# A two-block transformer on one core: the next batch's routed-row attention moved beside the causal attention's first half, and the second MLP beside the second half's maxima

## The reference, cut to what matters

```python
h = _layernorm(x) * (1 + ca) + sa
x = x + ga * (light_attn(h) + scatter(null_token, idx_q, heavy_attn(h[idx_q], h[idx_kv])))
h = _layernorm(x) * (1 + cb) + sb
x = x + gb * (einsum(relu(s[..., None] * W1 + b1), W2) + b2) @ Wout      # s = h @ Win + bin
h = _layernorm(x) * (1 + ca1) + sa1
x = x + ga1 * causal_attention(h)       # q, k normalised per head, rotary, softmax, 16 heads of 16
h = _layernorm(x) * (1 + cb1) + sb1
x = x + gb1 * (gelu(h @ bw1.T + b1) @ bw2.T + b2)                        # binarised weights
```

## Time and profile before

| | us |
|---|---|
| median of three runs | 5111.87 |
| the profiled execution's own time | 5113.72 |
| its span, first to last instruction | 5112.0 |
| TensorE matmul busy | 3773.6 (74%) |
| VectorE (DVE) busy | 2667.1 (52%) |
| ScalarE (ACT) busy | 2000.5 (39%) |
| GpSimd (POOL) busy | 1505.8 (29%) |
| mean granted TensorE clock | 0.854 of full |

### The profile page before, as it was taken

How to read it: one execution, slowest core, us unless ns; L and a number is a source line. 1 busy time by engine, 2 the same in 40 slices (tenths; PEclk the granted TensorE clock), 3 DMA queues, 4 the chain that set the end, 5 groups by cost and what they waited for, 6 DMA issues and landing times. The chain is left out here.

```text
span 5112.0 us, 59839 instructions
## 1 busy us (share of the span) xinstructions
PE 3773.6 (74%) x19064; PEld 2104.3 (41%) x19064; DVE 2667.1 (52%) x7124; ACT 2000.5 (39%) x4464; POOL 1505.8 (29%) x1900
## 2 busy tenths in 40 slices
PE   2014956789768877788768977789768977789777
PEld 1012633346333553346433543346333543346333
DVE  3845454635645364635645364636545364636542
ACT  0040433344425443345425443345425443345433
POOL 0611333124331343114321343114321343114311
PEclk7556968899779987899779988899779988899789
DMA  4200012100220013100120012100220012100220
GB/s 139 90 27 27 11 38 68 29 12 19 45 70 13 19 38 68 29 12 19 45 70 13 19 38 68 29 12 19 45 70 13 19 38 68 29 12 19 45 51 5
DMA packets 207220, 191.49 MB, mean 37 GB/s; under 512 B 12825, under 2 KB 189081, under 8 KB 206874
## 3 DMA queue, kind: packets, MB, share of 16 engines
q1 hardware_dynamic: 189378, 161.19, 12.8%
q10 hardware_dynamic: 14208, 18.09, 1.0%
q0 software_dynamic: 3328, 8.39, 0.6%
HBM read 121.99 MB, written 65.11 MB: 37 GB/s over the span
## 5 line engine op out<-in xcount | busy, mean ns | idle before, releaser
L2120 ACT ACTIVATE arena<-pb 128x512 f32<-128x512 f32 (+3 forms) x1536 | 679.2, 491 | 683.4 <-PE pb L1375 678.6
L2203 POOL TENSOR_TENSOR arena<-arena,small 128x512 f32<-128x512 f32 x256 | 279.8, 1094 | 641.1 <-DVE small L1553 638.8
L1952 ACT ACTIVATE arena<-arena,small 128x256 f32<-128x256 f32 x512 | 256.0, 500 | 451.2 <-DVE small L1536 451.1
L2361 POOL TENSOR_SCALAR_AFFINE_SELECT arena<-arena 128x256 f32<-128x256 f32 x512 | 212.2, 419 | 711.7 <-ACT arena L2120 708.3
L1375 PE MATMUL pb<-arena 98*128 98x512 bf16 (+3 forms) x1152 | 355.1, 352 | 81.4 <-DMA arena<-nullv_nmr 50.5
L1392 PE MATMUL pb<-arena,v 128*17 128x512 f32 (+3 forms) x3072 | 384.1, 513 | 22.6 <-POOL arena L2361 12.7
L1823 DVE TENSOR_REDUCE arena<-pb 128x1 f32<-128x512 f32 x512 | 328.4, 681 | 103.6 <-PE pb L1350 103.5
L1815 DVE TENSOR_REDUCE arena<-pb 128x4 f32<-128x512 f32 x256 | 174.3, 691 | 371.8 <-PE pb L1341 366.9
L1089 PE MATMUL pb<-arena 128*128 128x256 f32 x1024 | 291.3, 409 | 11.8 <-issue 6.3
L1536 DVE CUSTOM_DVE_ANT_0 arena<-pb,wmask 128x256 f32<-128x256 f32 x512 | 195.9, 419 | 198.7 <-PE pb L1089 152.1
L1066 PE MATMUL pb<-hTf,wqkv 128*128 128x512 f32 (+1 forms) x640 | 262.4, 553 | 35.8 <-issue 22.9
(11 more groups left out here) (340 smaller groups left out, 7889.1 us busy)
## 6 DMA issues: line engine op xcount, KB each, us to landing
split_q<-arena SPq DMA_DIRECT2D x384, 64.0 KB
arena<-split_q SPq DMA_DIRECT2D x64, 384.0 KB, 4.5
split_k<-arena SPq DMA_DIRECT2D x192, 64.0 KB
arena<-split_k SPq DMA_DIRECT2D x24, 384.0 KB, 15.9
arena<-in_x SPq DMA_DIRECT2D x8, 1024.0 KB, 7.7
h_d<-arena ACTq DMA_DIRECT2D x8, 1024.0 KB, 4.4
xn<-h_d SPq DMA_DIRECT2D x8, 1024.0 KB
xt<-in_x SPq DMA_DIRECT2D x16, 512.0 KB, 3.9
```

Source lines behind the costliest of these rows:

```text
L1952: ins = s.activation(pm[n % 3][:, j], sm[n % 2][:, j], ACT.Exp, bias=nmx[:, 2 * sl + j:2 * sl + j + 1], scale=-1.0, accum_out=sml[:, 2 * s ...
L2120: s.activation(pp[pn % 4][:, h % 2, 0:w_], bank[n % 3][:, 0:w_], ACT.Exp).then_inc(a_exp1, 1)
L2203: g.tensor_tensor(pm[n % 3], pm[n % 3], rcl[:, 2 * sl:2 * sl + 2].unsqueeze(2).broadcast_to([P, 2, 2 * P]), ALU.mult).then_inc(p_norm0, 1)
L2361: g.affine_select(out=p2, in_=p2, pattern=[[0, 2], [1, P]], compare_op=ALU.is_ge, fill=0.0, base=0, channel_multiplier=-1).then_inc(p_tri, 1)
```

## The change

It moves stages in the planner and adapts what they wait for:

- lane 1 takes heavy of batch b+1 directly after chain 2, ahead of mlp1 of the first half, gated on chain 3's end; heavy gets 71 steps instead of 61;
- while heavy is under way beside att, lane 0's pace is 0.28 (PACE_BESIDE_HEAVY); otherwise 0.5 beside the first half and 1.0 beside the second (before 0.9 and 0.8);
- the second half may begin without mlp1 of the first half; hnorm starts at att step 45 instead of 1;
- the gathers leave mlp1 and stand at heavy's start on GpSimd, one a step, behind the wait for chain 3's last part; heavy's waits for the MLP's last products go;
- the loads of the second half's first two head groups leave chain 3's end and att's start, and stand at key tile 2 of groups 2 and 3 of the first half.

Stepping the new `schedule()` gives for a middle batch: chains 2 and 3 end at att steps 11 and 19 of the first half; heavy stands beside steps 20 to 37 and the first 2 of the second half; mlp1 of the first half beside steps 3 to 27 (the fills); hnorm beside 53 to 62; mlp1 of the second half beside the next light, as before. In batch 0 heavy's ten more steps stand beside light, ahead of the chains.

```diff
-    "heavy": 61, "chain": 42, ("mlp1", 0): 25, ("mlp1", 1): 24, "hnorm": 10,
+    "heavy": 71, "chain": 42, ("mlp1", 0): 25, ("mlp1", 1): 24, "hnorm": 10,
-PACE = {("light", 0): 1.5, ("light", 1): 1.0, ("att", 0): 0.9, ("att", 1): 0.8}
+PACE = {("light", 0): 1.5, ("light", 1): 1.0, ("att", 0): 0.5, ("att", 1): 1.0}
+PACE_BESIDE_HEAVY = 0.28
...
-        lanes[1] += [("heavy", b, 0)] * (b == 0) + [("chain", b, 0), ("chain", b, 2), ("mlp1", b, 0)]
-        lanes[1] += [("heavy", b + 1, 0)] * (b + 1 < B) + [("mlp1", b, 1)]
+        lanes[1] += [("heavy", b, 0)] * (b == 0) + [("chain", b, 0), ("chain", b, 2)]
+        lanes[1] += [("heavy", b + 1, 0)] * (b + 1 < B) + [("mlp1", b, 0), ("mlp1", b, 1)]
-            gate["hnorm", b, 0] = [(("att", b - 1, 1), 1)]
+            gate["hnorm", b, 0] = [(("att", b - 1, 1), 45)]
+            gate["heavy", b, 0] = [(("chain", b - 1, 3), 42)]
-        gate["att", b, 1] = [(("chain", b, 2), 42), (("chain", b, 3), 42), (("mlp1", b, 0), 14)]
+        gate["att", b, 1] = [(("chain", b, 2), 42), (("chain", b, 3), 42)]
...
+            if lanes[0][0][0] == "att" and lanes[1] and lanes[1][0] in done and lanes[1][0][0] == "heavy":
+                pace = PACE_BESIDE_HEAVY
...
                 def heavy(b, _):                      # DVE
                     if b:
-                        v.wait_ge(t_w2, TH * (2 * b - 1))
-                        v.wait_ge(p_w2, TH * (2 * b - 1))
-                        v.wait_ge(split_out[1][1], 16 * SPLIT_DMAS * b)
+                        v.wait_ge(split_out[1][0], 16 * SPLIT_DMAS * b)
...
+                    if b:
+                        v.wait_ge(p_chain[1], nth(CHAIN_P, 2 * b - 1, "lo1"))
...
                 def gather(b):                        # GpSimd
+                    if b:
+                        g.wait_ge(split_out[1][0], 16 * SPLIT_DMAS * b)
+                        g.wait_ge(p_chain[1], nth(CHAIN_P, 2 * b - 1, "lo1"))
...
                 def heavy(b, _):
+                    yield from gather(b)
                     g.wait_ge(gate01_in, 16 * (b + 1))
                     if b:
-                        g.wait_ge(t_w2, TH * (2 * b - 1))
                         g.wait_ge(split_out[1][1], 16 * SPLIT_DMAS * b)
...
-                    if c == 0 and b + 1 < B:          # GpSimd, mlp1
-                        g.wait_ge(t_n2, 4 * b + 2)
-                        g.wait_ge(p_chain[1], nth(CHAIN_P, 2 * b + 1, "lo1"))
-                        gather(b + 1)
...
-                    if q == 3:                        # SyncE, chain
-                        load_group(b, 1, 0)
...
-                        if c == 0 or g > 0:           # SyncE, att
+                        if c == 0 or g == 2:
                             load_group(b, c, g)
...
+                            if c == 0 and g >= 2 and kt_ == 2:
+                                load_group(b, 1, g - 2)
```

More of the change, by code:

```diff
@@ L102, in schedule @@
             gate["start", b, 0] = [(("hnorm", b, 0), 10)]
-            gate["hnorm", b, 0] = [(("att", b - 1, 1), 1)]
+            gate["hnorm", b, 0] = [(("att", b - 1, 1), 45)]
+            gate["heavy", b, 0] = [(("chain", b - 1, 3), 42)]
         for q in range(4):
             light = ("light", b, q // 2)
-            gate["chain", b, q] = [(("heavy", b, 0), 61), (light, steps_of(light) - (2 if q % 2 else 18))]
+            gate["chain", b, q] = [(("heavy", b, 0), steps_of(("heavy", b, 0))), (light, steps_of(light) - (2 if q % 2 else 18))]
             if b:
@@ L126, in turn @@
             return
-        if key[0] == "chain" and key[2] == 3 and n == 41 and not reached([(("chain", key[1], 2), 42), (("att", key[1], 0), 22)]):
+        if key[0] == "att" and key[2] == 0 and n == NEXT_KEYS and not reached([(("chain", key[1], 2), 42), (("chain", key[1], 3), 42)]):
             return
-        if key[0] == "light" and key[1] > 0 and key[2] == 0 and n == LOAD_STEP and not reached([(("heavy", key[1], 0), 61)]):
+        if key[0] == "light" and key[1] > 0 and key[2] == 0 and n == LOAD_STEP and not reached([(("heavy", key[1], 0), steps_of(("heavy", key[1], 0)))]):
             return
@@ L1136, in heavy @@
                 def heavy(b, _):
-                    yield
-                    yield
+                    for _ in range(12):
+                        yield
                     for j in range(4):
@@ L1981, in heavy @@
                 def heavy(b, _):
-                    yield
-                    yield
+                    for _ in range(12):
+                        yield
                     if b:
-                        s.wait_ge(p_w2, TH * (2 * b - 1))
                         s.wait_ge(split_out[1][1], 16 * SPLIT_DMAS * b)
@@ L2239, in heavy @@
                     yield
-                    for j in range(4):
+                    for j in range(6):
                         yield
@@ L2449, in heavy @@
                     load_gates(b, 0, 2, gate01_in)
+                    for _ in range(11):
+                        yield
                     sp.wait_ge(p_const, 2 * b + 1)
                     sp.dma_start(heavy_d.rearrange("(t p) d -> p t d", p=P), nullg.unsqueeze(1).broadcast_to([P, T, D])).then_inc(fill_in, 16)
-                    for _ in range(60):
+                    for _ in range(59):
                         yield
@@ L2490, in chain @@
                     yield
-                    if q == 3:
-                        load_group(b, 1, 0)
-                        if b + 1 < B:
-                            for j_ in range(2):
-                                sp.wait_ge(t_chain[j_], nth(CHAIN_T, n, "p_n2"))
-                            sp.dma_start(xn[:, :, :], h_d[(b + 1) * N:(b + 2) * N, :].rearrange("(t p) d -> p t d", p=P)).then_inc(in_h, 16)
+                    if q == 3 and b + 1 < B:
+                        for j_ in range(2):
+                            sp.wait_ge(t_chain[j_], nth(CHAIN_T, n, "p_n2"))
+                        sp.dma_start(xn[:, :, :], h_d[(b + 1) * N:(b + 2) * N, :].rearrange("(t p) d -> p t d", p=P)).then_inc(in_h, 16)
                     yield
```

7 lines of the change are left out of this document (5 added, 2 removed).

## The result

| | before | after |
|---|---|---|
| median, us | 5112.63 (5106.52 to 5113.86) | 5299.35 (5288.02 to 5315.81, 4 runs) |
| ratio to before | | 1.037, 95% interval 1.034 to 1.040 |
| profiled execution, us | 5113.72 | 5315.81 |
| TensorE busy, us | 3773.6 | 3905.6 |
| mean granted clock | 0.854 | 0.842 |

The change costs 187 us where 112 were forecast. The median lies 4 us above the forecast's own range (5165 to 5295) and 11 inside the range of 8 in 10 (5040 to 5310).

The account below looks back on a forecast made before the run. Outside the score steps, waits inside stages and program order bound a batch. -54.7 - 7 + 78 = +16.3 us a middle batch, seven +114, batch 7 -7, batch 0 +4: +111, 5225 us; own range 5165 to 5295, 8 in 10 5040 to 5310.

Parts of the forecast that it names:

- Second half: Second half of a middle batch: heavy and hnorm leave, -54.7 us; second MLP beside the fills, -7 us.
- Chains at double pace: First half up to att step 19: 75 us, with chain turns at 1.08 us each wherever they stand.
- Prelude: Heavy's gathers to transposes beside att steps 20 to 23 of the first half: 17 us, those steps hidden.
- Projections: Heavy's six rotations in the first half with four att steps half hidden beside them: 24 us.
- Rounds with heavy's end: Heavy's sixteen full rounds at 3.7 us, trailing rounds, projections and the attention's last steps in the first half: 76 us.
- Light: The light stage of each batch: not touched by the change, so no cost was forecast.
- Heavy fits the first half as well as the second: Rival, 28%: beside att steps 20 to 37 the move costs +55 us, not +78; kernel about 5060 us.
- The MLP gains nothing: Rival, 5%: program order holds MLP and fills, so their -7 us a batch becomes 0; kernel 5280 us.
- everything waits in turn: Rival, 9%: in the first half nothing of heavy is hidden, or half clock; +111 us, kernel 5450 us.
- wrong if rounds came under 4 us apart: Sign against the forecast: heavy's head rounds in the first half standing less than 4 us apart.
- 4.5 to 5 us apart: Expected sign: spacing of heavy's head rounds in the first half, against 6.5 us before the change.

Follow-up runs that it names:

- experiment 4: Kernel before with chains 2 and 3 at pace 0.5 instead of 0.9 beside the first half, nothing else: 5258.03 us, ratio 1.029.
- experiment 5: Kernel after with heavy's eight gathers issued in one step of GpSimd instead of one a step: 5318.47 us, ratio to before 1.040.
- experiments 1 and 2: Heavy's head rounds and their scatter left out for batches 1 to 7: 4936.21 us in the kernel before, 4968.20 us in the kernel after.
- 6 and 9: Kernel after with heavy's pace beside the attention at 0.5 and at 0.8 instead of 0.28: 5186.44 us and 5099.65 us.
- experiment 3: Kernel before without the gate that keeps the second half's fills behind 14 steps of the second MLP: 5150.50 us, ratio 1.009.
- gates early, second half 1.0: Kernel before with the next batch's gates loaded at chain 3's end and the second half's pace 1.0 instead of 0.8: 4997.93 us, ratio 0.979.

## Why the prediction came out, and where its sizes were off

The direction, the reason and the range held: taking heavy out of the second half saves less than it costs in the first. The size did not: a middle batch loses twice the forecast. By the prediction's own steps, for a middle batch, forecast +16.3 and measured 606.0 - 574.1 = +31.9:

- *Second half.* Forecast -61.7 for both terms; from heavy's end to the end of the scores there are 169.6 us (61.1 + 108.5) where 230.4 were, -60.8. Right, and the MLP's gain as well. hnorm in group 3 with the rest made the scores 108.5 instead of 106.8.
- *Chains at double pace.* Forecast 75 us to step 19, measured 82.3. This step failed in its reasoning: "the turns cost the same wherever they stand" at 1.08 us each on top of 12 us of fills. I had one point, 27.5 us, and split it as a sum. At that price 24.5 turns beside the fills come to 38.5 us, and took 47.9. For steps 14 to 19 the same prices give 34 us with the 12 turns that are there, and 34.4 were measured. The prediction counted 39 turns and there were 36.5, which hid part of the error. By itself the double pace cost 17.0 us a batch in experiment 4, of which the forecast had none.
- *Prelude.* Forecast 17, measured 31.4 on the mean of batches 1 to 6. I counted the attention's four steps as hidden behind it; by the trace of experiment 5 they set it, and one stood 5.05 us for the row of maxima's load, issued behind chain 3's four stores. I had named heavy's own chain and not the steps ahead of it.
- *Projections.* Forecast 24, measured 23.3 on the mean, 24.7 in batch 5.
- *Rounds with heavy's end.* Forecast 76, measured 63: a round took 2.7 to 3.4 us by batch (first to last round's scores, over 15) and not 3.7. The timeline of after shows them:

```profile
3911.72 1.12 PE L1207 MATMUL pb<-arena 128*64 128x128 f32 x4 [0.70 <-DVE arena L1650]
...
3915.95 1.11 PE L1207 MATMUL pb<-arena 128*64 128x128 f32 x4 [0.70 <-DVE arena L1650]
...
3920.92 1.12 PE L1207 MATMUL pb<-arena 128*64 128x128 f32 x4 [0.70 <-DVE arena L1650]
```

  Here, at half clock, they are 4.2 and, with an output transpose between, 5.0 us apart, near the 4.6 worked out for half clock; most others were at the full one. The wait for DVE's copies ahead of L1207 is the one that I named, at 0.7 us. By the prediction's own mark, "wrong if rounds came under 4 us apart", this term was wrong; the mark, and the "4.5 to 5 us apart" beside it, contradict the 3.7 of its sum.
- *Light.* "Light isn't touched": 5.1 us a batch longer, 220.6 against 215.5. The forecast put this at nothing. The planner writes light's steps and those beside them in another order in batches 1 to 4 (last section).

The sum: light 5.1, chains 7.3, prelude and projections 54.7 - 41 = 13.7, rounds -13, second half 0.9, and 1.3 since the old first half is 112.7 on the mean and not 114: 15.3 of the 15.6 us that the batch is off. Batches 0 and 7 came to +10 and +1 instead of +20 and -7. The wrong terms had both signs, and that the total stayed in the range is luck in part: with 76 us for the rounds, as forecast, seven batches would have been 91 us longer and the kernel some 5390.

The rivals. "Heavy fits the first half as well as the second" is false with 3.6 of its steps to one of attention: experiments 1 and 2 give 47 us a batch for the rounds against 25. Whether the pace or the place makes it false, no run tells. A lower pace in 6 and 9 also carries the rounds out of the first half, to the second half's fills and score steps, and moves the MLP. What they show is the sum: 113 and 200 us less with one round or fewer to a step, most of them beside fills, than with nearly two to a step beside the first half's last steps and its tail. (The rival's condition reads 85% busy "as beside the score steps"; the rows have 89%.) "The MLP gains nothing" is true of its gate alone (experiment 3) and false in the change. The half-clock form of "everything waits in turn" didn't come: the first half with heavy ran at 0.68 to 0.93.

On the clock the Trainium skill ("TensorE: Matmul & The Clock Gate", Part 1, the HAM clock gate) says that idleness brings half clock. The rows agree at the ends: 0.64 where the chains' waits leave TensorE busy for 58%, 1.00 where rounds and fills fill each other's gaps, with TensorE busy for 73% of the time. The busy share alone doesn't order them: heavy's end in after has 81% at 0.77.

## What to carry to other kernels

When two step lists are woven into one order, a price per step read from one stretch doesn't carry to another: an added turn of two chains cost 1.5 to 2 us beside fills, a turn of one chain 0.4 beside score steps and tail. Ask for each stretch which list sets the time, and get a second point before splitting one into a sum. Work with gaps in it was cheaper spread thinly over many steps of something dense than in a burst; the pace of the weave, with the places that move with it, was worth 200 us in one kernel and 84 in the other. And before an order is rebuilt, turn its existing knobs one by one: two small edits of the kernel before gave 2.1%, the rebuilt order lost 3.7%.

## What the runs showed of the hardware

Light's matmuls are the same in every batch, yet it has two times. It looks like two states of the chip, but the times follow the order in which the planner writes light's steps. `schedule()` never sets `credit` back, so what the earlier stages leave decides how light begins. With less than 2.0 when light issues its first step, light goes one step ahead of the MLP's first, and chains 0 and 1 start beside light's steps 43 and 60 (A). With 2.0 or more light goes two steps ahead, and the chains start beside steps 44 and 59 (B). Stepping each kernel's `schedule()` and measuring each batch's light in its trace gives:

```
light, us, batches 1 to 7
before                          216A 215A 215A 216A 215A 215A 215A
after                           225B 225B 224B 224B 213A 212A 212A
before, chains at double pace   221B 221B 213A 221B 220B 213A 220B
after, heavy at 0.8             214A 226B 214A 226B 214A 227B 214A
gates early, second half 1.0    216A 229B 229B 216A 227B 218A 218A
```

In the 14 traces there are 98 such lights: 59 of A take 211.6 to 218.5 us, 39 of B 219.4 to 229.3, without an overlap. No run changed this order alone. The first 218 matmuls of light in after, batch 3 (B) and batch 5 (A):

```profile
2333.10:2400.10 67.00, 61.62 (x217) 37.29 (x218) 17.23 (x53) 28.22 (x52) 13.14 (x12) 0.95 0.06 17
3548.20:3609.20 61.00, 59.09 (x218) 35.17 (x219) 17.53 (x54) 25.54 (x50) 13.48 (x13) 1.00 0.06 18
```

Here half of the 12 us arise, with a granted clock of 0.95 in place of 1.00. Over the whole of light the share of the clock that was not granted comes to (1 - 0.923) x 224.3 = 17.3 us against (1 - 0.946) x 212.7 = 11.5, so that about half of the difference shows in the clock. Why order B waits more is open. It is up to 13 us a batch, as much as most edits here are worth. So edits of a few us a batch can't be read from the total, only from the stage, and a new pace also changes stages that it doesn't name.
